# Filling products of an attention kernel as four column tiles, with another order of its steps

## Chip, core and metric

One core of a Trainium2 chip. The metric is the device time of one launch in microseconds, the median of three runs.

## What is computed

All in float32, for 4 sequences (batches) of 512 tokens with 256 features:

```
h   = x + up(relu(down(x)))           # both weights scaled and shifted by cond_512 of the batch
p   = sigmoid(h @ Wp + bp)            # 8 heads, 5 levels
sim = sum over levels of cumprod(pq*pk + (1-pq)*(1-pk)) / 5
x1  = x + (softmax(causal(sim)) @ (h @ Wv)) @ Wo
U   = cond_512 @ W_dec + b_dec        # 257 x 30 for each batch
y   = x1 @ (U[:-1] @ V) + U[-1] @ V
out = x1 + y + expert_w[argmax(y @ gate_w.T)] @ y
```

## The kernel before

Everything lies transposed in SBUF: features on partitions, tokens along the free axis. sim is an inner product of 32 features for each head and token: `feat` holds them, built on DVE (line 530) from tanh of the logits, PE transposes them (step phi, line 640), and scores is a product over 32 rows. The kernel does not form y in full: z = U.T x1 (30 numbers a token), the scores of the gate come from z, and the expert's output from z spread over eight places (`zo`), one of which is filled.

One list, `ORDER`, lies behind all five engines: each runs through it and issues its own part of every step, in that order, with semaphores between. The list is made of a prologue and, for each batch b, six pairs p (four heads g, one half of the queries, one or two blocks of keys). `ORDER` has scores(p+1), then what `after_scores(b)` names for this pair, then context(p), then what `after_context(b)` names. These filling steps belong to the next batch or to the one before:

- down (616, four products of x and w_dn with 64 columns of weights), its relu on ACT; up (624), its sum into `h_t` on DVE (439). One h_t serves all batches.
- VL(b, t) (634): values and logits of token block t, 296 columns, copied to `v_sb` by ACT (361). Full products, 128 rows and 128 columns of weights.
- bias (DVE 448), tanh (ACT 367), feat (DVE 527 to 534), phi (PE 640, ACT 374).
- U(0) to U(3) (654), four column tiles of 32 each; DVE copies them to `u_row` (465). After U(3) the SP queue sends u_row to DRAM and back as `u_raw` (285, 289), and Uadd (DVE 473) makes `u_w`. WoU (665) is wo times u_w, copied by DVE (478). ubT (659) is a transpose whose copy `ub_col` is DVE's (469). Q (646) and its four copies `q_bd` (454), G(0), G(1) (672) and `gexp` (482).
- zT (685): z of a batch, column tiles; zs (692, 693): its transpose and the gate's scores, with a chain of six operations on DVE (497 to 504). zo: POOL (336), for the last batch DVE (512). zoT(b, half) (700): four transposes, copied by ACT (386).
- out(b, i) (714): four products of 256 columns, two with wo, two with gexp, summed into x_t by DVE (519) and stored by SP (295).

context(p) (572, 577) is done as column tiles of 32: four heads side by side, once with the values and once with ones for the denominators. After the last pair of a half DVE normalises: a reciprocal (404) and a multiplication (405). scores(p+1) waits until ACT's exp (349) of pair p has emptied the four score banks; context(p) waits for that exp and, on the diagonal, for POOL's mask (328).

Filling steps after the prologue share two PSUM banks in turn (`WORK`): a step waits for the step two before it to be emptied (lines 598, 599). `mm` (539) is the helper of every product, so the profile gives line 539 for them. A float32 product is shown as two matmul instructions, two passes over its columns. Shapes are given as rows*columns of the array: 32*128 scores, 128*32 column tiles, 128*64 down, 64*128 up, 128*128 full products and transposes.

Of the kernel before, what the change touches and what calls it, by code (L numbers as in the profile page):

```python
# [10 lines left out]
P = 128  # L11
B, T, D = 4, 512, 256
TT = T // P
DC = D // P
HD = 64
H, DEPTH = 8, 5
DH = D // H
# [6 lines left out]
CW = 2 * P  # L24
# [39 lines left out]
ALL_T, FIRST, SECOND = (0, 1, 2, 3), (0, 1), (2, 3)  # L64
# [8 lines left out]
def after_scores(b):  # L73

    n1, prv = b + 1, b - 1
    gaps = [[] for _ in range(BP)]
    if n1 < B:
        gaps[0] += [("up", n1, 0), ("up", n1, 1)]
    if b == 0:
        gaps[1] += [("VL", n1, 2), ("VL", n1, 3)]  # L80
        gaps[2] += [("U", 1)]
        gaps[3] += [("U", 3)]
        gaps[4] += [("Q",), ("Uadd",)]
        gaps[5] += [("G", 1)]
    elif n1 < B:
        gaps[1] += [("VL", n1, 0), ("VL", n1, 1)]
        gaps[2] += [("VL", n1, 2), ("VL", n1, 3)]
    if b == 1:
        gaps[0] += [("WoU",)]
    if prv >= 1:  # L90
        gaps[0] += [("out", prv - 1, 3)]
    if prv >= 0:
        gaps[4] += [("zoT", prv, 1)]
        gaps[5] += [("out", prv, 1)]
    return gaps


def after_context(b):

    n1, n2, prv = b + 1, b + 2, b - 1  # L100
    gaps = [[] for _ in range(BP)]
    if b == 0:
        gaps[0] += [("VL", n1, 0), ("VL", n1, 1)]
        gaps[1] += [("bias", n1), ("tanh", n1), ("U", 0), ("feat", n1)]
        gaps[2] += [("U", 2)]
        gaps[4] += [("ubT",), ("G", 0)]
    if prv >= 0:
        gaps[1] += [("zT", prv, ALL_T)]
        gaps[2] += [("zs", prv, ALL_T), ("zo", prv, 0), ("zo", prv, 1)]
        gaps[3] += [("zoT", prv, 0)]  # L110
        gaps[4] += [("out", prv, 0)]
        gaps[5] += [("out", prv, 2)]
    if b >= 1 and n1 < B:
        gaps[2] += [("bias", n1), ("tanh", n1), ("feat", n1)]
    if n1 < B:
        gaps[3] += [("phi", n1, 0), ("phi", n1, 1)]
    if n2 < B:
        gaps[5] += [("down", n2)]
    if b == B - 1:
        gaps[2] += [("zT", b, FIRST)]  # L120
        gaps[4] += [("zs", b, FIRST), ("zo", b, 0)]
        gaps[5] += [("zoT", b, 0), ("out", prv, 3)]
    return gaps


ORDER = list(PROLOGUE)
for _b in range(B):
    for _i, (_a, _c) in enumerate(zip(after_scores(_b), after_context(_b))):
        _p = _b * BP + _i
        if _p + 1 < ALL:  # L130
            ORDER += [("scores", _p + 1)]
        ORDER += _a + [("context", _p)]
        ORDER += _c
ORDER += [("out", B - 1, 0), ("zT", B - 1, SECOND), ("zs", B - 1, SECOND), ("zo", B - 1, 1),
          ("out", B - 1, 1), ("zoT", B - 1, 1), ("out", B - 1, 2), ("out", B - 1, 3)]

NO_BANK = ("scores", "context", "bias", "tanh", "feat", "Uadd", "zo")
# [12 lines left out]
def build(nc, x_tr, first, lift, vl, mix, bp, W_dec, b_dec, expert_tr, out_tr):  # L150
    with ExitStack() as ctx:
# [17 lines left out]
        w_vl = sb("w_vl", [P, DC, D + H * DEPTH])  # L169
        mix_sb = sb("mix_sb", [P, 2 * DC * D + D + DC * P + DC * E])  # L170
        wo = mix_sb[:, 0:DC * D].rearrange("p (c n) -> p c n", c=DC)
        wo_t = mix_sb[:, DC * D:2 * DC * D].rearrange("p (c n) -> p c n", c=DC)
# [15 lines left out]
        w_dn = sb("w_dn", [P, B, DC, HD])  # L188
# [348 lines left out]
        def _(pe):  # L537
            def mm(o, w, r, start=True, stop=True):
                return nc.tensor.matmul(o, w, r, start=start, stop=stop, skip_group_check=True)  # L539

            def scores(p):

                b, (g, _, units, _, first, _) = pair(p)
                if p == 0:
                    for k in range(2, EARLY):
                        pe.wait_ge(emptied[k], EARLY_TURNS[k])
                else:
                    pe.wait_ge(exped, p)
                if p % BP < NG:
                    done(pe, ("phi", b, g))  # L550
                for i, (kt, q0, n) in enumerate(units):
                    for h in range(HG):
                        rows = slice(NF * h, NF * (h + 1))
                        ins = mm(s_ps[:, h, CW * i:CW * i + n], phi_t[rows, b % 2, g, P * kt:P * (kt + 1)],
                                 phi_t[rows, b % 2, g, q0:q0 + n])
                ins.then_inc(scored, 1)
# [27 lines left out]
            for s in ORDER:  # L584
# [23 lines left out]
                elif kind == "down":  # L608
# [2 lines left out]
                        done(pe, ("gdn", (0,) if b == 0 else (1, 2, 3)))  # L611
                    pe.wait_ge(ld_x[b], 16)
                    for c in range(DC):
                        for j in range(2):
                            ins = mm(o[HD * j:HD * (j + 1), 0:T // 2], w_dn[:, b, c, :],
                                     x_t[:, b, c, T // 2 * j:T // 2 * (j + 1)], start=(c == 0), stop=(c == DC - 1))
                elif kind == "up":

                    _, b, j = s
# [6 lines left out]
                elif kind == "VL":  # L626
# [4 lines left out]
                        done(pe, ("up", b, 0))  # L631
                        done(pe, ("up", b, 1))
                    for c in range(DC):
                        ins = mm(o[:, 0:D + H * DEPTH], h_t[:, c, P * t:P * (t + 1)], w_vl[:, c, :],
                                 start=(c == 0), stop=(c == DC - 1))
                elif kind == "phi":
                    _, b, g = s
                    pe.wait_ge(feat_ready, b + 1)
# [18 lines left out]
                elif kind == "ubT":  # L657
                    done(pe, ("U", 3))
                    ins = nc.tensor.transpose(o[:, 0:B], ub_row[:].rearrange("b j k -> b (j k)"), ident[0:B, 0:B])
                elif kind == "WoU":  # L660
                    pe.wait_ge(u_ready, 1)
                    pe.wait_ge(ld_mix, 16)
                    for c in range(DC):
                        for d in range(DC):
                            ins = mm(o[:, P * c:P * (c + 1)], wo_t[:, d, P * c:P * (c + 1)],
                                     u_w[:, d].rearrange("p b k -> p (b k)"), start=(d == 0), stop=(d == DC - 1))
                elif kind == "G":
                    pe.wait_ge(ld_mix, 16)
                    pe.wait_ge(ld_ex, 16)
                    for hc in range(DC):  # L670
                        for j in range(4):
                            ins = mm(o[KP * j:KP * (j + 1), 0:D], wt[:, P * hc:P * hc + KP],
                                     ex_t[:, 4 * s[1] + j, hc, :], start=(hc == 0), stop=(hc == DC - 1))
                elif kind == "zT":
                    _, b, ts = s
                    if b == 0:
                        done(pe, ("ubT",))
                        done(pe, ("WoU",))
                    pe.wait_ge(ctx_ready, BC * b + (NG if ts == FIRST else BC))
                    for c in range(2 * DC):  # L680
                        for t in ts:
                            tok = slice(P * t, P * (t + 1))
                            w = u_w[:, c, b, :] if c < DC else wo_u[:, c - DC, KP * b:KP * (b + 1)]
                            r = x_t[:, b, c, tok] if c < DC else ctx_t[:, b % 2, c - DC, tok]
                            ins = mm(o[KP * t:KP * (t + 1), 0:P], w, r, start=(c == 0), stop=(c == 2 * DC - 1))
                elif kind == "zs":
                    _, b, ts = s
                    done(pe, ("zT", b, ts))
                    if b == 0:
                        done(pe, ("Q",))  # L690
                    rows = slice(KP * ts[0], KP * (ts[-1] + 1))
                    nc.tensor.transpose(o[:, 0:KP * len(ts)], z_t[rows, :], ident[rows, rows])
                    ins = mm(o[:, P:P + len(ts) * E], z_t[rows, :],
                             q_bd[rows, ts[0]:ts[-1] + 1].rearrange("p t e -> p (t e)"))
                elif kind == "zoT":
                    _, b, hf = s
                    pe.wait_ge(zo_ready, 2 * b + hf + 1)
                    for e in range(2):
                        for i in range(2):
                            ins = nc.tensor.transpose(  # L700
                                o[:, CW * e + P * i:CW * e + P * (i + 1)],
                                zo[:, 2 * hf + i, 4 * e:4 * e + 4, :].rearrange("p e k -> p (e k)"), ident[:])
                elif kind == "out":
                    _, b, i = s
                    if b == 0 and i == 0:
                        done(pe, ("G", 0))
                        done(pe, ("G", 1))
                    row, half = slice(P * (i % DC), P * (i % DC + 1)), slice(CW * (i // DC), CW * (i // DC + 1))
                    for c in range(2 * DC):
                        if c == DC:  # L710
                            done(pe, ("zoT", b, i // DC))
                        w = wo[:, c, row] if c < DC else gexp[:, c - DC, row]
                        r = ctx_t[:, b % 2, c, half] if c < DC else zo_t[:, c - DC, half]
                        ins = mm(o[:, 0:CW], w, r, start=(c == 0), stop=(c == 2 * DC - 1))
                ins.then_inc(filled, 1)


# [38 lines left out]
```

## Time and profile before

| | |
|---|---|
| three runs | 169.91, 170.01, 173.27 us; median 170.01 |
| the profiled execution | 169.74 us, its span 167.3 us |
| PE busy | 149.8 us (90%), 1728 matmuls |
| DVE, ACT, POOL busy | 75.3, 58.9, 29.1 us |
| mean granted clock of PE | 0.99 |

Times in the rows are microseconds from the start of the span. A busy time of PE covers matmuls that overlap, and their ends are modelled; starts are recorded. In a row, "x8" counts merged instructions and the bracket is the idle time before, with what released it.

### The profile page before, as it was taken

To read this page: it belongs to the slowest core of one execution; us is meant where nothing else is said; L and a number is where in the kernel's file an instruction comes from. 1 tells how busy PE (TensorE), PEld (TensorE's weight loads), DVE (VectorE), ACT (ScalarE), POOL (GpSimd) and SP (SyncE) were. 2 spreads that over 40 slices of the span, in tenths; PEclk is the share of its full clock that TensorE was granted. 3 is DMA by queue.
4 is the path that set the end of the run, shared out by engine and by line. 5 is a ranking of instruction groups with operands and counts; after the bars stand their busy time and mean duration, and the time that the engine had idled before them with its cause. 6 is when DMAs were issued, how large, how long until landed. Compare 5 with 4: busy or idle time off the path is not lost.

```text
span 167.3 us, 3934 instructions
## 1 busy us (share of the span) xinstructions
PE 149.8 (90%) x1728; PEld 102.3 (61%) x1728; DVE 75.3 (45%) x148; ACT 58.9 (35%) x70; POOL 29.1 (17%) x56
## 2 busy tenths in 40 slices
PE   6989489999965899987999899968999999999893
PEld 6656255654733577555676577646776766667672
DVE  0570708086705854177026365086143754164341
ACT  3004353725730424554430334466223447301010
POOL 8000022003022100250220200250222025200000
PEclk9999999999999999997899999999999999999999
DMA  5999999000220000000000010000011000010111
GB/s 127 295 427 449 387 365 289 16 4 0 33 31 4 0 4 0 4 0 0 4 33 31 31 35 0 4 0 4 11 52 35 31 4 0 4 63 31 63 34 64
DMA packets 7376, 12.42 MB, mean 74 GB/s; under 512 B 1552, under 2 KB 5808, under 8 KB 7232
## 3 DMA queue, kind: packets, MB, share of 16 engines
q10 hardware_dynamic: 2496, 7.23, 11.1%
q1 hardware_dynamic: 4768, 4.89, 9.2%
q0 software_dynamic: 96, 0.05, 0.8%
q8 instruction: 14, 0.23, 0.6%
q14 instruction: 2, 0.02, 0.0%
HBM read 9.95 MB, written 2.22 MB: 73 GB/s over the span
## 4 chain that ended last, share of the span: by engine, by line
PE 76%; DVE 12%; DMA 4%; ACT 3%; issue 2%; SPq 1%; POOL 0%; POOLq 0%; DVEq 0%; ACTq 0%
PE work L539 35%; PE c_ps L539 21%; PE s_ps L539 15%; DVE feat L530 4%; DMA u_scratch<-u_row 2%; PE work L700 2%; DVE h_t L439 2%; DMA u_raw<-u_scratch 2%; PE work L640 1%; DVE rden L404 1%; ACT prob L349 1%; DVE u_w L473 1%; ACT phi_t L374 1%; DVE x_t L519 1%; SPq L285 1%
## 5 line engine op out<-in xcount | busy, mean ns | idle before, releaser
L349 ACT ACTIVATE prob<-s_ps 128x1536 f32<-128x1536 f32 (+1 forms) x24 | 38.2, 1591 | 36.1 <-PE s_ps L539 35.9
L404 DVE RECIPROCAL rden<-c_ps 128x256 f32<-128x256 f32 x16 | 28.1, 1757 | 20.0 <-PE c_ps L539 20.0
L328 POOL TENSOR_SCALAR_AFFINE_SELECT prob<-prob 128x1024 f32<-128x1024 f32 x16 | 18.1, 1132 | 107.1 <-ACT prob L349 107.1
L539 PE MATMUL c_ps<-prob,v_sb 128*32 128x256 f32 (+1 forms) x384 | 26.8, 351 | 0.0
L539 PE MATMUL s_ps<-phi_t 32*128 32x256 f32 (+1 forms) x384 | 24.9, 374 | 1.5 <-ACT phi_t L374 1.0
L539 PE MATMUL c_ps<-prob,ones 128*32 128x256 f32 (+1 forms) x384 | 26.1, 344 | 0.0
L539 PEld LDWEIGHTS s_ps<-phi_t 32*128 32x128 f32 x384 | 17.9, 190 | 9.3 <-issue 5.4
L519 DVE TENSOR_TENSOR x_t<-work,x_t 128x256 f32<-128x256 f32 x16 | 6.8, 423 | 29.3 <-PE work L539 29.3
L539 PE MATMUL work<-ctx_t,mix_sb 128*128 128x256 f32 x64 | 17.8, 401 | 1.2 <-DVE h_t L439 0.8
L539 PEld LDWEIGHTS c_ps<-prob,v_sb 128*32 128x32 f32 x384 | 10.3, 110 | 11.0 <-issue 4.3
L539 PE MATMUL work<-zo_t,gexp 128*128 128x256 f32 x64 | 16.5, 381 | 0.0
L539 PEld LDWEIGHTS c_ps<-prob,ones 128*32 128x32 f32 x384 | 12.2, 110 | 5.6 <-issue 0.2
L539 PE MATMUL work<-w_vl,h_t 128*128 128x296 f32 x52 | 14.8, 426 | 0.6 <-DVE h_t L439 0.6
L539 PEld LDWEIGHTS work<-ctx_t,mix_sb 128*128 128x128 f32 x64 | 11.0, 190 | 5.1 <-issue 1.8
L539 PEld LDWEIGHTS work<-zo_t,gexp 128*128 128x128 f32 x64 | 12.1, 190 | 1.8 <-ACT zo_t L386 0.2
L539 PEld LDWEIGHTS work<-w_vl,h_t 128*128 128x128 f32 x52 | 9.3, 190 | 4.5 <-issue 2.0
L386 ACT COPY zo_t<-work 128x512 f32<-128x512 f32 x8 | 4.7, 582 | 12.2 <-PE work L700 12.1
L530 DVE TENSOR_TENSOR feat<-feat,sign 128x64 f32<-128x64 f32 (+3 forms) x16 | 8.3, 522 | 0.5
L336 POOL TENSOR_TENSOR zo<-z_nat,pick 128x256 f32<-128x256 f32 x12 | 7.2, 627 | 7.4 <-DVE pick L504 7.4
L361 ACT COPY v_sb<-work 128x296 f32<-128x296 f32 x13 | 5.2, 403 | 8.1 <-PE work L539 8.1
L439 DVE TENSOR_TENSOR h_t<-work,x_t 128x512 f32<-128x512 f32 x6 | 3.9, 686 | 8.1 <-PE work L539 8.1
L405 DVE TENSOR_TENSOR ctx_t<-c_ps,rden 128x256 f32<-128x256 f32 x16 | 6.8, 425 | 0.6
(92 smaller groups left out, 120.1 us busy)
## 6 DMA issues: line engine op xcount, KB each, us to landing
wdec<-in_W_dec ACTq DMA_DIRECT2D x1, 3855.0 KB, 14.8
x_t<-in_x_tr SPq DMA_DIRECT2D x4, 512.0 KB, 9.2
ex_t<-in_expert_tr ACTq DMA_DIRECT2D x1, 2048.0 KB, 23.0
out_x<-x_t SPq DMA_DIRECT2D x16, 128.0 KB, 1.7
mix_sb<-in_mix ACTq DMA_DIRECT2D x1, 776.0 KB, 16.5
lift_sb<-in_lift ACTq DMA_DIRECT2D x1, 384.0 KB, 4.3
w_vl<-in_vl SPq DMA_DIRECT2D x1, 296.0 KB, 5.5
first_sb<-in_first SPq DMA_DIRECT2D x1, 144.0 KB, 4.0
```

The source lines that it names most:

```text
L328: nc.gpsimd.affine_select(out=tri, in_=tri, compare_op=ALU.is_ge, fill=0.0, base=0, pattern=[[0, HG], [0, 2], [1, P]], channel_multiplier= ...
L336: ins = nc.gpsimd.tensor_tensor(zo[:, t], z_nat[:, t:t + 1, :].broadcast_to([P, E, KP]), pick[:, t, :].unsqueeze(2).broadcast_to([P, E, KP ...
L349: nc.scalar.activation(prob[:, p % 2, :, 0:width(p)], s_ps[:, :, 0:width(p)], ACT.Exp).then_inc(exped, 1)
L361: nc.scalar.copy(v_sb[:, b % 2, t, :], bank(s)[:, 0:D + H * DEPTH]).then_inc(empty(s), 1)
L386: nc.scalar.copy(zo_t[:, :, CW * s[2]:CW * (s[2] + 1)], bank(s)[:].rearrange("p (e t) -> p e t", e=2)).then_inc(empty(s), 1)
L404: link(nc.vector.reciprocal(rden[:], c_ps[m % 2][:, CW:2 * CW]))
L405: nc.vector.tensor_tensor(ctx_t[:, b % 2, g, CW * half:CW * (half + 1)], c_ps[m % 2][:, 0:CW], rden[:], ALU.mult).then_inc(ctx_ready, 1)
L439: nc.vector.tensor_tensor(h_t[:, :, half], bank(s)[:].rearrange("p (c t) -> p c t", c=DC), x_t[:, b, :, half], ALU.add).then_inc(empty(s), 1)
L519: nc.vector.tensor_tensor(x_t[:, b, c, half], bank(s)[:, 0:CW], x_t[:, b, c, half], ALU.add).then_inc(empty(s), 1)
L530: ins = nc.vector.tensor_tensor(feat[:, :, n:2 * n], feat[:, :, 0:n], sign[:, :, i:i + 1].broadcast_to([P, TT * H, n]), ALU.mult)
L539: return nc.tensor.matmul(o, w, r, start=start, stop=stop, skip_group_check=True)
L700: ins = nc.tensor.transpose(o[:, CW * e + P * i:CW * e + P * (i + 1)], zo[:, 2 * hf + i, 4 * e:4 * e + 4, :].rearrange("p e k -> p (e k)") ...
```

## The change

The products of VL, WoU and out are issued through a new helper, `tiled`: each product of 128 columns of weights becomes four of 32 columns, with the same moving operand, each into its own 32 partitions of the bank. down takes 32 columns of weights in place of 64. And the filling steps change places: phi and zoT stand behind scores, zs too, with zo; Q goes to the place behind context(3), Uadd behind G(1), WoU behind down(2); zT goes one pair later or earlier, and out follows context in other pairs.

```diff
@@ -76,22 +76,20 @@
     gaps = [[] for _ in range(BP)]
     if n1 < B:
         gaps[0] += [("up", n1, 0), ("up", n1, 1)]
+        gaps[4] += [("phi", n1, 0), ("phi", n1, 1)]
     if b == 0:
         gaps[1] += [("VL", n1, 2), ("VL", n1, 3)]
         gaps[2] += [("U", 1)]
         gaps[3] += [("U", 3)]
-        gaps[4] += [("Q",), ("Uadd",)]
-        gaps[5] += [("G", 1)]
+        gaps[5] += [("G", 1), ("Uadd",)]
     elif n1 < B:
-        gaps[1] += [("VL", n1, 0), ("VL", n1, 1)]
+        gaps[1] += [("zs", prv, ALL_T), ("zo", prv, 0), ("zo", prv, 1), ("VL", n1, 0), ("VL", n1, 1)]
         gaps[2] += [("VL", n1, 2), ("VL", n1, 3)]
-    if b == 1:
-        gaps[0] += [("WoU",)]
-    if prv >= 1:
-        gaps[0] += [("out", prv - 1, 3)]
+    else:
+        gaps[1] += [("zs", prv, ALL_T), ("zo", prv, 0), ("zo", prv, 1)]
+        gaps[4] += [("zs", b, FIRST), ("zo", b, 0)]
     if prv >= 0:
-        gaps[4] += [("zoT", prv, 1)]
-        gaps[5] += [("out", prv, 1)]
+        gaps[3] += [("zoT", prv, 0), ("zoT", prv, 1)]
     return gaps
 
 
@@ -103,23 +101,23 @@
         gaps[0] += [("VL", n1, 0), ("VL", n1, 1)]
         gaps[1] += [("bias", n1), ("tanh", n1), ("U", 0), ("feat", n1)]
         gaps[2] += [("U", 2)]
-        gaps[4] += [("ubT",), ("G", 0)]
-    if prv >= 0:
-        gaps[1] += [("zT", prv, ALL_T)]
-        gaps[2] += [("zs", prv, ALL_T), ("zo", prv, 0), ("zo", prv, 1)]
-        gaps[3] += [("zoT", prv, 0)]
-        gaps[4] += [("out", prv, 0)]
+        gaps[3] += [("Q",)]
+        gaps[4] += [("G", 0), ("ubT",)]
+        gaps[5] += [("down", n2), ("WoU",)]
+    else:
+        gaps[0] += [("zT", prv, ALL_T)]
+        gaps[3] += [("out", prv, 0)]
+        gaps[4] += [("out", prv, 1)]
         gaps[5] += [("out", prv, 2)]
     if b >= 1 and n1 < B:
         gaps[2] += [("bias", n1), ("tanh", n1), ("feat", n1)]
-    if n1 < B:
-        gaps[3] += [("phi", n1, 0), ("phi", n1, 1)]
-    if n2 < B:
+    if prv >= 1:
+        gaps[1] += [("out", prv - 1, 3)]
+    if b >= 1 and n2 < B:
         gaps[5] += [("down", n2)]
     if b == B - 1:
         gaps[2] += [("zT", b, FIRST)]
-        gaps[4] += [("zs", b, FIRST), ("zo", b, 0)]
-        gaps[5] += [("zoT", b, 0), ("out", prv, 3)]
+        gaps[5] = [("zoT", b, 0), ("out", prv, 2), ("out", prv, 3)]
     return gaps
 
 
@@ -131,7 +129,7 @@
             ORDER += [("scores", _p + 1)]
         ORDER += _a + [("context", _p)]
         ORDER += _c
-ORDER += [("out", B - 1, 0), ("zT", B - 1, SECOND), ("zs", B - 1, SECOND), ("zo", B - 1, 1),
+ORDER += [("zT", B - 1, SECOND), ("out", B - 1, 0), ("zs", B - 1, SECOND), ("zo", B - 1, 1),
           ("out", B - 1, 1), ("zoT", B - 1, 1), ("out", B - 1, 2), ("out", B - 1, 3)]
 
 NO_BANK = ("scores", "context", "bias", "tanh", "feat", "Uadd", "zo")
@@ -538,6 +536,13 @@
             def mm(o, w, r, start=True, stop=True):
                 return nc.tensor.matmul(o, w, r, start=start, stop=stop, skip_group_check=True)
 
+            def tiled(o, w, r, start, stop):
+
+                for j in range(P // DH):
+                    part = slice(DH * j, DH * (j + 1))
+                    ins = mm(o[part], w[:, part], r, start=start, stop=stop)
+                return ins
+
             def scores(p):
 
                 b, (g, _, units, _, first, _) = pair(p)
@@ -611,9 +616,10 @@
                         done(pe, ("gdn", (0,) if b == 0 else (1, 2, 3)))
                     pe.wait_ge(ld_x[b], 16)
                     for c in range(DC):
-                        for j in range(2):
-                            ins = mm(o[HD * j:HD * (j + 1), 0:T // 2], w_dn[:, b, c, :],
-                                     x_t[:, b, c, T // 2 * j:T // 2 * (j + 1)], start=(c == 0), stop=(c == DC - 1))
+                        for j in range(4):
+                            ins = mm(o[DH * j:DH * (j + 1), 0:T // 2], w_dn[:, b, c, DH * (j % 2):DH * (j % 2 + 1)],
+                                     x_t[:, b, c, T // 2 * (j // 2):T // 2 * (j // 2 + 1)],
+                                     start=(c == 0), stop=(c == DC - 1))
                 elif kind == "up":
 
                     _, b, j = s
@@ -631,8 +637,8 @@
                         done(pe, ("up", b, 0))
                         done(pe, ("up", b, 1))
                     for c in range(DC):
-                        ins = mm(o[:, 0:D + H * DEPTH], h_t[:, c, P * t:P * (t + 1)], w_vl[:, c, :],
-                                 start=(c == 0), stop=(c == DC - 1))
+                        ins = tiled(o[:, 0:D + H * DEPTH], h_t[:, c, P * t:P * (t + 1)], w_vl[:, c, :],
+                                    start=(c == 0), stop=(c == DC - 1))
                 elif kind == "phi":
                     _, b, g = s
                     pe.wait_ge(feat_ready, b + 1)
@@ -662,8 +668,8 @@
                     pe.wait_ge(ld_mix, 16)
                     for c in range(DC):
                         for d in range(DC):
-                            ins = mm(o[:, P * c:P * (c + 1)], wo_t[:, d, P * c:P * (c + 1)],
-                                     u_w[:, d].rearrange("p b k -> p (b k)"), start=(d == 0), stop=(d == DC - 1))
+                            ins = tiled(o[:, P * c:P * (c + 1)], wo_t[:, d, P * c:P * (c + 1)],
+                                        u_w[:, d].rearrange("p b k -> p (b k)"), start=(d == 0), stop=(d == DC - 1))
                 elif kind == "G":
                     pe.wait_ge(ld_mix, 16)
                     pe.wait_ge(ld_ex, 16)
@@ -711,7 +717,7 @@
                             done(pe, ("zoT", b, i // DC))
                         w = wo[:, c, row] if c < DC else gexp[:, c - DC, row]
                         r = ctx_t[:, b % 2, c, half] if c < DC else zo_t[:, c - DC, half]
-                        ins = mm(o[:, 0:CW], w, r, start=(c == 0), stop=(c == 2 * DC - 1))
+                        ins = tiled(o[:, 0:CW], w, r, start=(c == 0), stop=(c == 2 * DC - 1))
                 ins.then_inc(filled, 1)
```

## Rows read from the trace of the kernel before

**Rows 1.** The profile page, chain that ended last, shares by engine.

```profile
PE 76%; DVE 12%; DMA 4%; ACT 3%; issue 2%; SPq 1%; POOL 0%; POOLq 0%; DVEq 0%; ACTq 0%
```

**Rows 2.** Waits of PE from 20 us: us in total, times, longest.

```profile
PE work L539 <- DVE ub_col L469: 3.1, 1, 3.1
PE work L539 <- DVE h_t L439: 1.5, 2, 0.8
```

**Rows 3.** Timeline of PE, tail: start, us (modelled), engine, line, operation.

```profile
149.94 1.13 PE L539 MATMUL work<-ctx_t,mix_sb 128*128 128x256 f32 x4
...
154.52 1.03 PE L539 MATMUL work<-ctx_t,mix_sb 128*128 128x256 f32 x4
155.38 1.02 PE L539 MATMUL work<-zo_t,gexp 128*128 128x256 f32 x4
156.34 0.63 PE L539 MATMUL work<-x_t,u_w 128*32 128x128 f32 x8
...
163.64 0.60 PE L539 MATMUL work<-zo_t,gexp 128*128 128x256 f32 x2
```

**Rows 4.** Timeline of PE, 60.5 to 66.2 us.

```profile
60.53 1.15 PE L539 MATMUL s_ps<-phi_t 32*128 32x256 f32 x16
61.61 2.26 PE L539 MATMUL work<-w_vl,h_t 128*128 128x296 f32 x8
63.80 0.64 PE L539 MATMUL c_ps<-prob,v_sb 128*32 128x256 f32 x8
64.25 0.61 PE L539 MATMUL c_ps<-prob,ones 128*32 128x256 f32 x8
64.69 0.40 PE L539 MATMUL c_ps<-prob,v_sb 128*32 128x128 f32 x8
64.90 0.40 PE L539 MATMUL c_ps<-prob,ones 128*32 128x128 f32 x8
65.12 0.62 PE L539 MATMUL work<-x_t,u_w 128*32 128x128 f32 x16
```

**Rows 5.** Timeline of DVE, 36 to 62 us.

```profile
41.54 0.63 DVE L465 COPY u_row<-work 128x480 f32<-128x480 f32 x1
42.62 1.76 DVE L404 RECIPROCAL rden<-c_ps 128x256 f32<-128x256 f32 x1 [0.44 <-PE c_ps L539]
...
45.00 0.69 DVE L454 COPY q_bd<-work 32x8 f32<-32x8 f32 x4 [0.16 <-PE work L539]
50.28 1.38 DVE L473 TENSOR_TENSOR u_w<-u_raw,bdec 128x120 f32<-128x120 f32 x2 [4.60 <-DMA u_raw<-u_scratch]
```

**Rows 6.** Timeline of PE, 73.5 to 84 us.

```profile
74.28 0.63 PE L700 MATMUL work<-ident,zo 128*128 128x128 f32 x4 [0.27 <-POOL zo L336]
76.48 1.19 PE L640 MATMUL work<-ident,feat 128*128 128x128 f32 x8 [1.57 <-DVE feat L530]
...
82.30 1.13 PE L539 MATMUL work<-ctx_t,mix_sb 128*128 128x256 f32 x4
```

**Rows 7.** Timeline of DVE, 71 to 77 us.

```profile
71.54 0.29 DVE L497 COPY z_nat<-work 128x128 f32<-128x128 f32 x1 [3.95 <-PE work L539]
...
72.64 0.19 DVE L504 TENSOR_TENSOR pick<-key,kmax 128x32 f32<-128x32 f32 x1
```

**Rows 8.** Busy time by windows: us, PE, PEld, DVE, ACT, POOL, PEclk, DMA.

```profile
73.87:77.28 3.41, 1.57 (x20) 1.25 (x12) 3.31 (x5) 1.94 (x3) 1.46 (x3) 1.00 0.00 0
77.28:80.69 3.41, 3.41 (x30) 2.18 (x32) 1.15 (x2) 2.49 (x4) 0.00 (x0) 0.50 0.00 0
```

**Rows 9.** Timeline of PE, 110.5 to 118 us, the next batch.

```profile
113.48 1.06 PE L640 MATMUL work<-ident,feat 128*128 128x128 f32 x8 [1.57 <-DVE feat L530]
...
117.79 0.48 PE L539 MATMUL work<-ctx_t,mix_sb 128*128 128x256 f32 x1
```

**Rows 10.** Groups of instructions by shape: two of ACT.

```profile
L349 ACT ACTIVATE prob<-s_ps 128x2048 f32<-128x2048 f32 x8 | 15.0, 1873 | 15.4 <-PE s_ps L539 15.4
...
L386 ACT COPY zo_t<-work 128x512 f32<-128x512 f32 x8 | 4.7, 582 | 12.2 <-PE work L700 12.1
```

## The prediction

> **What bounds the kernel now.** The chain that ended last comes first: 76% of it is PE and only 12% DVE [rows 1]. So time is lost or won on PE: in its passes, in what lies between them, and in its waits. The list of PE's waits names the longest of the last kind [rows 2]: 3.1 us in one wait for ub_col, 1.5 us in two for h_t; those for feat come below. The PE timeline, read by start times, gives the rest.
>
> A float32 product takes two passes. In full products (128*128) a block of four passes of 256 columns is 154.52 to 155.38 = 0.86 us, 0.216 us a pass [rows 3]; in column-tiled ones (128*32, eight instructions = two passes by four tiles) 64.25 to 64.69 is 0.43 for two passes of 256, again 0.216, and 64.69 to 64.90 two of 128 columns at 0.109 us [rows 4]. So a pass costs the same either way. What differs is the change of shape. From 60.53 to 61.61 four passes (0.862) take 1.08: 0.21 us for entering scores (0.104) and leaving them (0.11). VL, 61.61 to 63.80: 8 passes of 0.249 = 1.99 of 2.19, so 0.20 for entering (0.105) and leaving (0.094). Tiled entry costs 0.025 (63.80 to 64.25 is 0.45 for 0.431), and from a context product to the tiled filling product there is nothing at all: 64.90 to 65.12 is 0.22, two passes [rows 4]. Leaving a full block once more: 155.38 to 156.34 is 0.96 against 0.864 [rows 3].
>
> **The change, part by part.**
>
> 1. Tiling. From scores(0) on I counted the blocks in the two orders as they are written out. Before: PE enters a full product block (VL, out, WoU) 17 times and leaves one 17 times; after, none, since each lies against a context or another tiled block. 17 x (0.105 + 0.094) = 3.4 us. Blocks of down lose their own 64-column shape: 3 x (0.05 + 0.10) = 0.45 us by 0.10 as leaving cost and 0.05 as entry, between the tiled and the full one. Transposes and Q make two more entries (0.06) and three more exits (0.094): +0.4 us. Context is left once less, 0.1. Sum: **-3.5 us**. The passes stay: 216 passes are turned into four-tile ones (16 VL x 4, 16 out x 8, WoU 8, down 16), 632 more matmul instructions beside the 1728, at no time each, because context passes of the same length show none. Bounds for the added instructions: below, nothing (no row has a pass shorter than its columns); above, 0.027 us each (four in a 128-column pass of 0.109 [rows 4]), 17 us, if nothing overlapped. I take nothing, the nearest row being exactly this shape; what no row shows is four tiles that read the same moving operand (a rival below).
>
> 2. Uadd behind G(1). Today ub_col stands behind Uadd on DVE, Uadd waits for u_raw to come back through DRAM, and G(1) waits for ub_col's bank: u_row's last copy ends at 42.17, Uadd starts at 50.28, 8.1 us [rows 5]. PE loses 3.1 us [rows 2]. After, PE has G(1), context(5), down(2) to do and only then WoU, which needs u_w. Is the transfer late then? From the end of U(3) the PE does context(3) 1.3, Q 0.6, scores(5) 0.75, phi with its new wait 2.3, context(4) 1.75, G(0) 0.86, ubT 0.4, scores(6) 0.85, G(1) 0.9: about 9.8 us; the transfer takes 1.1 (to the end of u_row's copy) + 8.1 = 9.2. So it has landed when DVE has emptied G(1). **-3.1 us.** WoU also leaves the place behind up(2), where it waited 0.85 us for h_t, and out(0,3) leaves that behind up(3), the same: **-1.6 us** (0.77 each in the list, 0.08 more by starts).
>
> 3. Transposes behind the scores, features two contexts later. Today zoT(b,0) waits 0.27 us idle (0.34 by starts) for zo, and phi starts 2.20 after it where four 128-column passes need 0.44 and 0.03: 1.74 lost [rows 6], and the same for the next batch. After, feat has scores(10), zoT, context(9), out(0,0), scores(11), over 6 us of PE, for its chain of bias, tanh and features, which today takes from the last pick of zs, 72.83 [rows 7], to the start of phi, 76.48: 3.65 us. zo today lets zoT start 1.45 us after that pick; after, it has 9 us. 2 x (0.34 + 1.74) = **-4.2 us**.
>
> 4. Clock. It is at half (0.50, 1.2 GHz) from 77.28 to 80.69, after a stretch 73.87 to 77.28 in which PE ran 1.57 us, nearly all of it transposes [rows 8]. What it costs: phi to out takes 76.48 to 82.30 = 5.82 [rows 6], and the same steps of the next batch 113.48 to 117.79 = 4.31 [rows 9]: 1.51 us. After, no such stretch is left behind the prologue: the longest without matmuls other than transposes is phi(1) with its wait, 2.3 us. **-1.5 us.**
>
> 5. The tail. From 149.94 to 163.64 are 13.70 us; in them lie 5.5 out products (9.5 us), two zoT (0.87), zT (0.87), zs (0.2): 11.45 [rows 3]. The rest is 2.25, of which some 0.6 are shape changes counted above, and 1.65 waits; before 149.94 one more of 0.45 (out(2,1) behind the zs block). After, out(3,0) covers z_t, and 0.3 us of waits are left: **-1.8 us**.
>
> 6. New waits. A result is in PSUM 0.18 us after the next pass starts (the block at 64.90 ends, as modelled, at 65.30, where the next has started at 65.12 [rows 4]); with 0.05 for the semaphore, an estimate, I take 0.23 for all. normalise is 2.21: the reciprocal starts at 42.62 and its multiply is over at 44.84, where q_bd's 0.16 of idle begins [rows 5]; 1.76 of it is the reciprocal, so 0.42 the multiply, and I take 0.42 for every DVE copy or sum of that shape.
>  - phi(1,1) takes the bank of Q, whose q_bd copies (0.69 [rows 5]) stand behind normalise of context(3): 0.23 + 2.21 + 0.69 + 0.06 = 3.19 after context(3); PE arrives after 0.11 + 0.40 + 0.09 + 0.75 + 0.11 + 0.49 = 1.97. **+1.2**.
>  - up(2,1) takes WoU's bank. On DVE behind G(1): 0.23 + 0.42 + Uadd 1.38 + normalise 2.21 + copy 0.42 + 0.06 = 4.7; PE: context 1.3, down 0.86, WoU 0.88, scores 0.75, changes 0.23 = 4.0. **+0.7**.
>  - VL(b,1) takes the bank of zs, whose chain of DVE (1.29, 71.54 to 72.83 [rows 7]) stands behind normalise: 0.23 + 2.21 + 1.29 + 0.06 = 3.8 to 3.9 against zT, scores, zs, VL(b,0) = 3.5. **+0.9** in two batches (0.46 each with the pieces unrounded).
>  - out(b,0) takes the bank of zoT(b,0), whose copy (0.58) stands behind the wide exp (1.87) on ACT [rows 10]: 0.23 + 1.87 + 0.58 + 0.06 = 2.74 against 2.46 of PE. 0.29 three times, **+0.9**.
>  - VL(1,0) comes 0.1 earlier to the h_t it waits for: **+0.1**.
>  Sum +3.8. The ends: half of it (1.9), if DVE and ACT are ahead of my walk, and twice (7.6), since each wait is the difference of two larger sums. The masks on POOL are no new wait: where context now stands right behind short scores, a whole tiled out before it covers exp and mask.
>
> Sum: -3.5 - 3.1 - 1.6 - 4.2 - 1.5 - 1.8 + 3.8 = -11.9. The profiled execution took 169.74 us, a span of 167.3 and 2.4 around it; the median is 170.01, 0.3 higher. 169.74 - 11.9 = 157.8 for the profiled one, 158.1 for the median. I say **158.0**.
>
> **Rivals.**
> - The clock falls all the same, in another place (the prologue, where PE waits for feat of batch 0, or the 2.3 us at phi(1)): +1.5, 159.5. For: the drop came once in this trace, and one of the three runs is 3.3 us above the others. Against: nothing so empty is left. 14%.
> - The waits move rather than go: DVE work of normalise, zs and features now meets in the same intervals, and the new waits are twice what I walked through: +3.8, 161.8. For: DVE's order is fixed and normalise is 2.2 us of it. Against: DVE is 12% of the chain. 10%.
> - The tiling does nothing (full products hid their entry, or four-tile ones pay it again): +3.5, 161.5. Against: 64.90 to 65.12 [rows 4]. 5%.
> - The other side: the four tiles of one product do not run beside each other as those of context do, since they read the same moving operand. If one tile's weight load or start showed in each added instruction at 0.027 us [rows 4], 632 x 0.027 = +17, 175 us. It decides from 11.9 / 632 = 0.019 us per added instruction. Against: context and U passes show under 0.001. 3%. The Trainium skill (TensorEngine Tiling, Instruction Overhead) speaks for it: it gives about 60 cycles of overhead to each matmul, so that 632 more would be an estimated 16 us (0.025 us each at 2.4 GHz) and the time near 174; the 0.43 us of eight instructions with 256 columns leave no room for it there.
>
> **Numbers.** My forecast has 68%. Its own range is 156 to 160; the clock and the moved waits stretch it to 161.5. Low end: half the new waits, 156.1, and a little more. A measurement of this kernel tells 2% (3.4 us) from no change, so faster is below 166.6: 0.95; same 0.02; slower 0.03.
>
> **What would show it.** Right: VL, out, WoU and down as 128*32, no gap between them and c_ps; about 2360 matmuls; the wait for ub_col gone and those for feat too; PEclk at full throughout; new idle before ident,feat near 45 us (1.2), before act_t near 55 (0.7). Wrong: a four-tile pass of 256 columns longer than 0.216 us; ub_col or u_w still waited for over 1 us; a half-speed stretch.

## The result, and the profile after

The changed kernel takes 156.82 us (median of four runs, 156.56 to 157.54), against 171.64 for the kernel before on the same chip in the same rounds (169.91 to 173.29); the ratio is 0.923, 95% interval 0.918 to 0.929. The forecast was 158.0, its range from a little below 156.1 to 161.5. The ratio leaves out the two executions of before at 173.3, which lost more of TensorE's clock than the others, and so it shows less than the two medians do. The profiled execution took 156.72 us, span 154.3.

From the page of the kernel after: busy time by engine, PEclk over the span, and the chain by engine.

```profile
PE 144.7 (94%) x2360; PEld 91.8 (59%) x2360; DVE 73.2 (47%) x148; ACT 58.8 (38%) x70; POOL 29.2 (19%) x56
...
PEclk9999999999999999999999999999999999999999
...
PE 88%; DVE 6%; ACT 2%; issue 1%; POOL 0%; POOLq 0%; DVEq 0%; ACTq 0%
```

PE has 632 more matmuls and is busy 5 us less. The chain runs over PE for 88% of the span where it was 76% [rows 1]; DMA is no longer in it.

The waits of PE from 20 us on:

```profile
PE s_ps L537 <- ACT phi_t L372: 1.0, 1, 1.0
PE work L646 <- DVE q_bd L452: 1.0, 1, 1.0
PE s_ps L537 <- ACT prob L347: 0.6, 1, 0.6
PE work L537 <- DVE pick L502: 0.5, 2, 0.2
```

ub_col and h_t [rows 2] are gone from it, and the waits of 1.57 us idle for feat [rows 6] too. Two of the four are the start of the pipeline and stood there before (phi_t and prob). The other two are new, and both had been forecast: q_bd and zs's pick. The list goes by idle time; a wait under some 0.2 us shows only as a later start.

The timeline of PE, first a stretch of context(11), out, down and scores, then the tail:

```profile
81.04 0.40 PE L537 MATMUL c_ps<-prob,ones 128*32 128x128 f32 x8
81.26 1.05 PE L537 MATMUL work<-ctx_t,mix_sb 128*32 128x256 f32 x16
82.13 1.05 PE L537 MATMUL work<-zo_t,gexp 128*32 128x256 f32 x16
82.99 1.05 PE L537 MATMUL work<-x_t,w_dn 128*32 128x256 f32 x16
83.97 0.94 PE L537 MATMUL s_ps<-phi_t 32*128 32x256 f32 x16
...
138.63 1.07 PE L537 MATMUL work<-ctx_t,mix_sb 128*32 128x256 f32 x16
...
150.57 1.05 PE L537 MATMUL work<-zo_t,gexp 128*32 128x256 f32 x16
```

Read it by starts. 81.04 to 81.26 is two passes of 128 columns, so nothing lies between context and out, nor between out and down. 81.26 to 82.13 and 82.13 to 82.99 are 0.865 for four passes: the 0.216 us of the full products [rows 3], although sixteen instructions stand where four stood and four tiles read the same moving operand. Only the step to scores, 82.99 to 83.97 = 0.98, has its 0.11 for leaving a shape. The tail from out(2,2) to the start of the last four passes is 11.9 us; it was 13.7 [rows 3], with one zoT (0.44 us) in it that now lies before.

### The profile page after: what moved, and what is told of

Its sections match the earlier page's. It is cut to its first block, busy times and chain, and to the rows that moved or that the text cites. A ratio compares the mean times of both kernels' runs of the same rounds, so it can differ in the third digit from the quotient of the medians.

```text
span 154.3 us, 5198 instructions
## 1 busy us (share of the span) xinstructions
PE 144.7 (94%) x2360; PEld 91.8 (59%) x2360; DVE 73.2 (47%) x148; ACT 58.8 (38%) x70; POOL 29.2 (19%) x56
## 4 chain that ended last, share of the span: by engine, by line
PE 88%; DVE 6%; ACT 2%; issue 1%; POOL 0%; POOLq 0%; DVEq 0%; ACTq 0%
PE work L537 38%; PE c_ps L537 27%; PE s_ps L537 18%; PE work L706 3%; PE work L646 2%; DVE rden L402 1%; DVE feat L528 1%; ACT prob L347 1%; DVE h_t L437 1%; ACT phi_t L372 1%; PE work L698 1%; DVE x_t L517 1%; PE s_ps L646 0%; DVE z_nat L495 0%; DVE q_bd L452 0%
## 5 line engine op out<-in xcount | busy, mean ns | idle before, releaser
L537 PE MATMUL s_ps<-phi_t 32*128 32x256 f32 (+1 forms) x384 | 24.2, 365 | 1.6 <-ACT phi_t L372 1.0
L537 PEld LDWEIGHTS s_ps<-phi_t 32*128 32x128 f32 x384 | 17.4, 184 | 10.6 <-issue 7.0
L537 PE MATMUL work<-ctx_t,mix_sb 128*32 128x256 f32 x256 | 17.0, 381 | 0.2
L537 PE MATMUL work<-zo_t,gexp 128*32 128x256 f32 x256 | 16.9, 379 | 0.0
L537 PEld LDWEIGHTS c_ps<-prob,v_sb 128*32 128x32 f32 x384 | 10.9, 109 | 8.7 <-issue 2.5
L537 PE MATMUL work<-w_vl,h_t 128*32 128x296 f32 x208 | 14.8, 416 | 1.1 <-DVE h_t L437 0.6
L537 PEld LDWEIGHTS work<-zo_t,gexp 128*32 128x32 f32 x256 | 8.6, 110 | 5.2 <-ACT zo_t L384 0.2
L537 PEld LDWEIGHTS work<-ctx_t,mix_sb 128*32 128x32 f32 x256 | 7.8, 109 | 4.9 <-ACT zo_t L384 0.8
L537 PEld LDWEIGHTS work<-w_vl,h_t 128*32 128x32 f32 x208 | 6.1, 109 | 7.1 <-DVE pick L502 1.6
L528 DVE TENSOR_TENSOR feat<-feat,sign 128x64 f32<-128x64 f32 (+3 forms) x16 | 6.5, 408 | 0.5
```

The source lines that it names most:

```text
L528: ins = nc.vector.tensor_tensor(feat[:, :, n:2 * n], feat[:, :, 0:n], sign[:, :, i:i + 1].broadcast_to([P, TT * H, n]), ALU.mult)
```

## The experiments

All times are medians. So that the start-up, which varies between executions (the first scores product starts at 20.6 to 22.2 us), does not blur the comparison, I also give a PE stretch for each profiled execution: from the first scores product to the start of the last four passes of out, both read from the PE timeline. It is 142.52 us for before (21.12 to 163.64) and 129.31 for after (21.26 to 150.57), and a second profiled execution of after gives 129.31 again. So a tenth of a microsecond counts between kernels with the order of after and a full clock. Where PE waits for ub_col, in the order of before, the end of a DRAM transfer is in the stretch too: that wait is 3.07, 3.21, 3.26 and 3.26 us of idle in four profiled executions, so 0.2 counts for nothing there.

**The two halves alone.** First the tiling, in the order of before:

```
the order functions and ORDER of before, with tiled() for VL, WoU and out, and down with 32 columns
```

> The order of before with the tiled products of after. Theory (shape changes cost 0.2 us for each block of full products, and nothing else of tiling counts): 3.0 to 3.5 us less than before, 166.5 us where before has 170.0; the waits for ub_col (3.1 us) and for feat (two of 1.6 us) stand as they were. Rival (tiling pays only where the order puts the blocks against context): about 1 us less, 169. Rival (four instructions for one cost time of their own): slower than before, 171 or more.

Measured 166.96 us (165.82 to 168.46), before 169.88 on that chip; ratio 0.981, interval 0.971 to 0.991. ub_col (3.2 us) and feat (3.2 in two) are waited for as before (3.1 each). The medians are 2.9 apart, and the interval reaches to 0.991, so times alone do not settle the size. The PE stretch is 140.39, but this execution spent 6.83 us at half clock where before's spent 3.41. With 1.5 us for each 3.41 (see the clock, below) that is 137.4 against 141.0: an estimated 3.6 us for the tiling. The starts bear the correction out: G(1), context and down take 6.03 us at half clock here (52.62 to 58.65), and 3.17 at full clock in after. Runs with the same mean clock differ by 3.0 us (two at 0.979 against two of before) and by 4.0 (two at 0.99 against four). The first theory holds; the gain does not need the new order.

Then the order, with full products:

```
the order functions and ORDER of after, with mm() for VL, WoU and out, and down with 64 columns
```

> The order of after with the full products of before (and down with 64 columns). Theory: after plus the shape changes, 3.1 us more than after, 159.9 us, clock full throughout. Rival (the order only moves waits, and most of the 13 us is tiling): 165 us or more. The two parts taken alone should add up, within 0.5 us, to the whole difference of the profiled runs, if each acts by itself.

Measured 160.29 us (159.40 to 160.65); PE stretch 132.66, 3.35 more than after. The clock is full. The same stretch of its timeline as above:

```profile
81.52 0.40 PE L537 MATMUL c_ps<-prob,ones 128*32 128x128 f32 x8
81.86 1.13 PE L537 MATMUL work<-ctx_t,mix_sb 128*128 128x256 f32 x4
82.82 1.03 PE L537 MATMUL work<-zo_t,gexp 128*128 128x256 f32 x4
83.78 1.08 PE L537 MATMUL work<-x_t,w_dn 128*64 128x256 f32 x8
```

81.52 to 81.86 is 0.34 where after has 0.22, and 81.86 to 82.82 is 0.96 where after has 0.87: leaving one shape and entering the next, twice 0.1 us. The two parts add up: 3.6 for tiles and, without the clock, 141.0 - 132.7 = 8.3 for order make 11.9, and the whole is 141.0 - 129.3 = 11.7, within the 0.5 that had been expected.

**Which part of tiling pays.** After, with tiles of 64 columns for VL, WoU and out:

```diff
-                for j in range(P // DH):
-                    part = slice(DH * j, DH * (j + 1))
+                for j in range(P // HD):
+                    part = slice(HD * j, HD * (j + 1))
```

> After, with VL, WoU and out split into two tiles of 64 columns instead of four of 32; down stays at 32. Theory (what counts is that filling products have the shape of the context products): each block enters for 0.05 and leaves for 0.10 again, 16 blocks, 2.4 to 2.8 us more than after, 159.4 us. Rival (what counts is narrow weights, whose load of 110 ns for 32 columns is hidden where 190 ns for 128 is not): half of the gain stays within the blocks and the time is 157.5 us or less. Rival (instructions cost): faster than after by half of what four tiles cost.

Measured 159.07 us (158.81 to 159.14), PE stretch 131.81, 2.50 more than after.

```profile
81.64 0.40 PE L537 MATMUL c_ps<-prob,ones 128*32 128x128 f32 x8
81.98 1.08 PE L537 MATMUL work<-ctx_t,mix_sb 128*64 128x256 f32 x8
82.89 1.03 PE L537 MATMUL work<-zo_t,gexp 128*64 128x256 f32 x8
83.85 1.07 PE L537 MATMUL work<-x_t,w_dn 128*32 128x256 f32 x16
```

Tiles as such bring little: 81.64 to 81.98 is 0.34 again, the block enters for 0.05 (0.91 for 0.865) and leaves for 0.10 (82.89 to 83.85). Of the 3.35 us between full products and after, two tiles of 64 bring 0.85, and a part of that is down's. What pays is that the filling product has the very shape of the context product beside it. That two, four or one instruction carry a pass is not seen.

**Uadd put back.** After, with Uadd ahead of G(0) and ubT:

```diff
-        gaps[5] += [("G", 1), ("Uadd",)]
+        gaps[5] += [("G", 1)]
...
-        gaps[4] += [("G", 0), ("ubT",)]
+        gaps[4] += [("Uadd",), ("G", 0), ("ubT",)]
```

> After, with Uadd put back ahead of G(0) and ubT, so that DVE waits for u_raw before it empties their banks. Theory (only the transfer's landing counts, some 8.1 us after the last copy of u_row at 42.1, so at 50.2): G(1), which starts at 49.6 in after, is held until about 51.2, 1.5 us more, 158.3 us. Rival (the whole 3.1 us of the old wait return, since the wait is one of order and not of time): 159.9 us. Rival (the transfer is early enough now): no change, 156.8 us.

Measured 158.49 us (158.21 to 159.23), PE stretch 131.25: 1.94 more than after. PE and DVE there:

```profile
52.11 1.07 PE L537 MATMUL work<-ex_t,mix_sb 128*32 128x256 f32 x16 [1.86 <-DVE gexp L480]
```

```profile
51.12 0.48 DVE L471 TENSOR_TENSOR u_w<-u_raw,bdec 128x120 f32<-128x120 f32 x2 [5.22 <-DMA u_raw<-u_scratch]
```

The wait comes back, but as 1.9 us and not the 3.1 of before [rows 2], since the new order reaches this point with more of the transfer's time already spent. It stands between the theory's 1.5 and the rival's 3.1, much nearer to the theory. The start-up of this execution lay 0.6 us later, and the transfer probably with it.

**The clock.** Two kernels fill idle time of before with work that has no result: the waits for feat of the batches 2 and 3, once with products, once with transposes.

```diff
+                    if b >= 2 and g == 0:
+                        for _ in range(6):
+                            mm(o[:, 0:P], ident[:], ident[:])
                     pe.wait_ge(feat_ready, b + 1)
```

> Before, with six products of the identity with itself (128 columns, two passes each, 1.3 us together, written to the bank that the transposes overwrite) ahead of the wait for feat, for the batches 2 and 3. They add no result and fill idle time only. Theory (the clock fell in before because the stretch ahead held hardly any products): full clock throughout, 1.5 us less in the profiled execution, 168.3 us; runs of before at 173.3 have two more such drops, and this kernel's runs all lie near 168.3. Rival (the drop has another cause, and the gain of after came from elsewhere): PEclk shows the drop again, 170.0 us.

> The same place filled with twelve transposes of the identity, as many passes (1.3 us) as in the kernel with products. If transposes do not count as activity for the clock, as the Trainium skill says (TensorE: Matmul & The Clock Gate, Part 4), the clock can fall as in before: 170 us, and runs near 173. If any work of PE counts, the time is that of the kernel with products, 168.3 us.

Products: 169.01 us (167.26 to 171.95, ten runs); transposes: 168.67 (167.15 to 169.80, ten runs); before 169.69 (167.49 to 171.55, nineteen). By time neither is told from before (both intervals hold 1). By the granted clock of each run, five of ten with products and six of ten with transposes held 1.00, and three of before's nineteen. The profiled execution with products had a full clock, as the theory had it, at 168.73 us and a PE stretch of 141.06, 1.46 less than before. But the other runs spread as before's do, and both theories were too narrow: the clock can fall after more than one stretch. Windows of three profiled executions show where it did (columns as in rows 8; 0.50 is 1.2 GHz, 1.00 is 2.4). The kernel with tiles only, the one filled with transposes, and the next one, with both stretches filled:

```profile
48.24:51.65 3.41, 1.17 (x24) 0.72 (x16) 0.66 (x2) 1.45 (x1) 0.65 (x1) 1.00 0.32 36
51.65:58.48 6.83, 5.86 (x64) 2.96 (x64) 2.94 (x5) 0.00 (x0) 0.58 (x1) 0.50 0.01 2
```

```profile
49.76:53.17 3.41, 1.19 (x24) 0.76 (x28) 1.88 (x5) 0.48 (x1) 1.10 (x1) 1.00 0.03 7
53.17:56.58 3.41, 3.41 (x38) 1.90 (x32) 1.53 (x2) 0.00 (x0) 0.00 (x0) 0.50 0.00 0
```

```profile
17.86:21.27 3.41, 1.58 (x10) 0.86 (x8) 3.13 (x9) 0.53 (x2) 0.00 (x0) 1.00 0.90 384
21.27:28.10 6.83, 6.00 (x44) 4.03 (x46) 0.21 (x1) 3.38 (x5) 1.09 (x1) 0.50 1.03 356
```

Before each fall PE had been busy 1.2 to 1.6 us of 3.4, as in [rows 8]; the places are G(1)'s wait for ub_col, twice, and the prologue's wait for the first features. So two more kernels fill the wait for ub_col too, with twelve products or 24 transposes:

```diff
+                if kind == "G" and s[1] == 1:
+                    pe.wait_ge(ctx_ready, 3)
+                    for _ in range(12):
+                        mm(c_ps[0][:, 0:P], ident[:], ident[:])
```

> The kernel with products in the waits for feat, and twelve more (2.6 us) in the wait of G(1) for ub_col, written to the context bank that is free there. In the traces so far the clock fell after the one stretch or after the other, by where it lay in that execution. Theory: with both stretches filled no execution loses clock, the profiled one shows 1.00, the median is 168.4 and the runs lie within 1 us or so of it, while those of before reach 171.5. Rival (the spread of before's runs is not the clock, but the inputs' transfers or the DRAM round trip): the runs spread over 3 to 4 us as before, at the same median as with the one fill, 169 us.

> The kernel with both stretches filled, with transposes of the identity in place of the products (24 and twice 12, the same number of passes). With products, 10 of 11 executions held a granted clock of 1.00, where 3 of 17 of before did on that chip. Theory (any work of PE keeps the clock, transposes as well): again nearly all executions at 1.00 and a median of 167.9 us. Rival, the rule of the Trainium skill (TensorE: Matmul & The Clock Gate, Part 4) that transposes do not count: the stretches are as empty as before, most executions at 0.98 or 0.99 and a median of 169.9 us.

Products in both: 167.87 us (167.35 to 171.24), before 169.88 (167.67 to 174.78). Every run lists its granted clock: ten of eleven held 1.00 (167.35 to 168.98 us), and the one that did not lost it in the prologue, which is not filled. Of before's seventeen runs there three held 1.00 (167.67 to 168.81), and the others go down to 0.96 at 174.78. Transposes in both: 168.34 us, four of five runs at 1.00 (0.999 in one), the fifth again with its fall in the prologue; before 171.19 and one of seven. So the theory of both expectations holds for these two stretches, with the prologue as an exception that neither had: work there keeps the clock, and in these counts transposes serve as well as products. Over all fills with transposes, ten of fifteen executions held 1.00, where four of 26 of before did on the same chips. The rule of the Trainium skill (TensorE: Matmul & The Clock Gate, Part 4) that transposes do not count as activity does not fit here: 4 of 5, where the unfilled kernel has 1 of 7. Five runs are few, and the ten of the single fill point the same way.

**Q early.** After, with Q between U(3) and context(3):

```diff
-        gaps[3] += [("U", 3)]
+        gaps[3] += [("U", 3), ("Q",)]
...
-        gaps[3] += [("Q",)]
```

> After, with Q moved from behind context(3) to between U(3) and context(3), so that its four copies on DVE stand ahead of normalise and not behind it. Theory (the 1.2 us before phi(1,1) are q_bd's place in DVE's order): this wait goes, 1.1 to 1.2 us less, 155.6 us; a part may return as a wait for u_w, since PE comes to WoU earlier (52.67 in after, Uadd over at 51.6). Rival (the wait moves on to u_w or to a bank): within 0.3 us of after, 156.6 us.

Measured 156.23 us (156.10 to 156.61); PE stretch 128.83, only 0.48 less than after. The wait for q_bd is gone from the list. The result lies between theory and rival: the rival was right that part of the wait moves on, and the rows show to where:

```profile
50.61 1.10 POOL L325 TENSOR_SCALAR_AFFINE_SELECT prob<-prob 128x1024 f32<-128x1024 f32 x1 [3.58 <-ACT prob L346]
```

```profile
50.73 1.31 DVE L470 TENSOR_TENSOR u_w<-u_raw,bdec 128x120 f32<-128x120 f32 x2 [0.23 <-DMA u_raw<-u_scratch]
```

```profile
54.02 1.66 PE L536 MATMUL work<-act_t,w_up 64*128 64x256 f32 x8
55.60 0.64 PE L536 MATMUL c_ps<-prob,v_sb 128*32 128x256 f32 x8
```

Uadd takes 1.31 us where the mask has started 0.12 ahead of it; in after it takes 0.47 and starts 0.2 ahead of the mask. So WoU starts 0.15 late (52.14, behind down at 51.12), normalise and WoU's copy are late too, and up with its switch takes 1.58 us where 1.07 is its own time and 1.20 what it took in after.

**VL(b,1) behind context**, on top of Q early:

```diff
-        gaps[1] += [("zs", prv, ALL_T), ("zo", prv, 0), ("zo", prv, 1), ("VL", n1, 0), ("VL", n1, 1)]
+        gaps[1] += [("zs", prv, ALL_T), ("zo", prv, 0), ("zo", prv, 1), ("VL", n1, 0)]
...
+    if b >= 1 and n1 < B:
+        gaps[1] += [("VL", n1, 1)]
```

> The kernel with Q early, and VL(b,1) of the batches 2 and 3 put behind context in place of ahead of it, so that zs's bank is long empty. Theory: two waits of 0.45 us go and no shape change comes: 0.9 us less than the one with Q early, 154.7 us. Rival (bias and feat come later and phi waits for them): the same as with Q early or slower.

Measured 155.05 us (154.92 to 155.22), PE stretch 127.76: 1.07 less. The waits for pick are gone, as the theory had it.

**The mask after Uadd**, on top of both:

```diff
                     pool.wait_ge(exped, p + 1)
+                    if p == BP:
+                        pool.wait_ge(u_ready, 1)
```

> The kernel with Q and VL(b,1) moved, and POOL's mask of pair 6 made to wait until Uadd is done; context(6), which needs this mask, comes 4 us later. Theory (DVE's Uadd, whose operands all lie in SBUF, crawls at 1.31 us while POOL works on the mask, and takes 0.47 alone): Uadd is back at 0.47 us, WoU and up(2,1) come 0.15 and up to 0.7 earlier, 0.5 to 0.7 us less than 155.05: 154.5 us. Rival (Uadd is slow for a reason of its own, such as late bytes of the transfer): it takes 1.3 us again and nothing changes, 155.1 us.

> The kernel after, unchanged, on the same chip and in the same rounds as the kernel with the late mask, as the reference for it. Theory: 156.8 us, runs within 1 us, clock 1.00 in the profiled execution; the ratio of before to it is again 0.92. A drop of the clock in any execution would put that run at 158.3 or more.

Measured 154.93 us (154.45 to 155.78), and after on the same chip 156.86 (156.49 to 157.58), before 169.88: ratios to before 0.919 (0.915 to 0.924) and 0.931 (0.927 to 0.935). The profile shows the mechanism:

```profile
49.74 0.48 DVE L474 TENSOR_TENSOR u_w<-u_raw,bdec 128x120 f32<-128x120 f32 x2
```

Uadd is back at 0.48 us (1.38 in the kernel without this edit), up at 1.19, and the PE stretch is 127.37, 0.39 less, under the 0.5 to 0.7 expected. On the medians alone this last step is not shown (155.05 on another chip). Together the three edits are worth 1.9 us over after.

## Why the prediction was right, by its steps

1. **Tiling, -3.5.** Measured 3.35 (order alone against after) and an estimated 3.6 (tiles alone). The passes and prices were as read, the count was not: by its starts before has 19 stretches that hold VL, WoU or out from 20 us on, and not 17, so some 0.3 us more of shape changes. A part came back as longer waits: out(b,0) waits 0.19 us in after, and 0.08 with full products in the same order. The added instructions cost nothing, which also settles the rival of four tiles with one moving operand: a pass of 256 columns takes 0.216 us in one, two or four instructions. The Trainium skill (TensorEngine Tiling (Array Packing), Instruction Overhead) gives each matmul an overhead of about 60 cycles. Added to each instruction, as the rival had it, it is not seen here; that a matmul of one column takes as long as one of 60, as the section goes on, no run here tests.
2. **Uadd behind G(1), -3.1; h_t, -1.6.** All three waits are gone; by starts they were 3.15 and 1.70. Put back in the new order, Uadd costs 1.9, so the worth of this move depends on the rest of the order. h_t was not tried by itself.
3. **Features, -4.2.** Both feat waits and the two for zo are gone, 4.16 by starts. This move was not tried by itself.
4. **Clock, -1.5.** Right for the profiled execution (1.46 by the fill, in which ub_col was waited for 0.2 longer) but too narrow as an account of the kernel: before loses clock in most executions, by their mean clocks of 1.00 to 0.96 none to four times over 3.4 us, if each costs 0.01 as in the profiled one; after in none of its ten. Between executions at full clock the gain is 167.85 to 156.86 = 11.0 us (median of before's three on the last chip of after). What single executions of before take above that, up to 6.9 us at 0.96, is for the most part clock (an estimated 6 us, four times 1.5).
5. **Tail, -1.8: too large.** 13.70 less the 0.44 that moved is 13.26, now 11.94. But with full products in the new order the same tail is 12.27 (141.01 to 153.28, below), so 0.33 is tiling, which step 1 has already, and the order brings 0.99. Ahead of the tail, out(2,1) started 0.47 behind the last zs product, and the same step takes 0.27 at 158.04: 0.2 of wait, not 0.45. Together 1.2.
6. **New waits, +3.8: mis-sized.** phi(1,1) measured 1.18 (forecast 1.2: 43.78 to 45.40 below, for 0.44), VL(b,1) 0.43 each (0.46) and VL(1,0) 0.1 (0.1). But up(2,1) lost 0.13 and not 0.7, and out(b,0) 0.19 each and not 0.29 (71.32 to 71.73 below is 0.41, where two such passes take 0.22). The sum is 2.9.

The timelines of PE and, below, ACT in after, and last the tail of PE with order alone:

```profile
43.78 0.66 PE L646 MATMUL work<-ident,feat 128*128 128x128 f32 x4
45.40 0.66 PE L646 MATMUL work<-ident,feat 128*128 128x128 f32 x4 [0.96 <-DVE q_bd L452]
...
54.52 1.26 PE L537 MATMUL work<-act_t,w_up 64*128 64x256 f32 x8
55.72 0.64 PE L537 MATMUL c_ps<-prob,v_sb 128*32 128x256 f32 x8
...
71.32 0.40 PE L537 MATMUL c_ps<-prob,ones 128*32 128x128 f32 x8
71.73 1.07 PE L537 MATMUL work<-ctx_t,mix_sb 128*32 128x256 f32 x16
```

```profile
69.32 1.88 ACT L347 ACTIVATE prob<-s_ps 128x2048 f32<-128x2048 f32 x1 [1.60 <-PE s_ps L537]
71.10 1.07 ACT L384 COPY zo_t<-work 128x512 f32<-128x512 f32 x2
```

```profile
141.01 1.03 PE L537 MATMUL work<-ctx_t,mix_sb 128*128 128x256 f32 x4
...
153.28 1.03 PE L537 MATMUL work<-zo_t,gexp 128*128 128x256 f32 x4
```

up: the term "Uadd 1.38" was taken from a row beside which POOL's mask ran (50.42 to 51.52) [rows 5]; with the mask behind it Uadd is 0.47. And up(2,0), whose bank is free, starts while up(2,1) still waits. out: two operations of ACT in a row overlap, the copy starting 0.10 before exp's end, where the sum had them one after the other. These two terms were 0.6 and 0.3 too large.

The profiled executions differ by 13.0 us, the PE stretches by 13.2, where the sum has 11.9. The new waits are 0.9 of this distance, the tail goes the other way with 0.6, and ub_col and h_t were 0.15 larger than their terms. Of the 0.8 or so left 0.3 are the two stretches that were not counted; the rest is open. So the mechanisms were right, but that the forecast lies within 1.2 us of the median is in part luck: errors of opposite sign in the terms.

The rivals: none decided. The clock did not fall elsewhere in the ten executions of after, the new waits were smaller than walked and not twice, and the tiling does what it says.

## What to carry to other kernels

On PE, give small filling products the array shape of their neighbours before looking for wider ones: here a full product between other shapes cost 0.2 us, a pass cost the same in any shape, and more instructions for a pass were free. Judge a wait by what stands ahead of the releasing operation in its engine's own order, and take that operation's duration from a row with the same neighbours. And where one to three microseconds of idle PE time stand together, look for the clock behind them: here it fell there in some executions and not in others, for some 1.5 us with each 3.4 at half speed.

## What had not been expected of the hardware

- DVE operations with both inputs in SBUF are held up by POOL, where POOL's started first. Uadd: 1.38 us for two with the mask starting between them [rows 5], 1.31 with the mask 0.12 ahead, 0.48 once the mask is made to wait. In after Uadd starts first, at 51.10, and keeps its 0.47 although the mask runs from 51.30; there the mask takes 1.23 us in place of 1.10. The last batch's zo on DVE takes 0.42 us each, but 1.37 for the one that starts 0.01 after a mask (the rows below, from after: both are over in 1.70). Four feature products take 2.64 us in before where POOL's zo runs beside them (73.70), and 1.74 in after, where POOL is idle (67.99). The reciprocal, which reads PSUM, has 1.76 us also at 52.06 in after, where the mask is still running. The Trainium skill (GPSIMD Engine Reference, 1. Specifications) names contention with DVE instructions that have two SBUF inputs; these runs agree.

```profile
134.43 1.70 DVE L510 TENSOR_TENSOR zo<-z_nat,pick 128x256 f32<-128x256 f32 x2
```

```profile
134.42 1.10 POOL L326 TENSOR_SCALAR_AFFINE_SELECT prob<-prob 128x1024 f32<-128x1024 f32 x1 [7.97 <-ACT prob L347]
```

- Transposes keep the clock as well as products do, in the two stretches tried (4 of 5 and 10 of 11 executions at 1.00).
- A kernel without long idle stretches on PE is also steadier: ten executions of after lie within 1.1 us, seventeen of before on one chip within 7.1.
